# Taking two more chunks of the first layer's activations off TensorE's transposes and through DRAM

## The chip, the cores and the metric

The kernel runs on one NeuronCore of one Trainium2 chip. The metric is device time in microseconds (us) for one execution; lower is better. TensorE (PE) does the matrix products and can also transpose, VectorE (DVE), ScalarE (ACT) and GpSimd (POOL) do element work, and SyncE (SP) issues most of the DMAs.

## What is computed

The input x has 64 batches of 32 channels by 512. Four residual layers follow each other. The first is the largest: a gated feed-forward layer with low-rank adapters chosen per batch.

```python
def L0(x, W_gate, W_up, W_down, A_gate, B_gate, A_up, B_up, A_down, B_down, ids):
    gate = x @ W_gate.T + 0.5 * adapters(x, A_gate, B_gate, ids)     # F = 1376 columns
    up   = x @ W_up.T   + 0.5 * adapters(x, A_up, B_up, ids)
    act  = silu(gate) * up
    return act @ W_down.T + 0.5 * adapters(act, A_down, B_down, ids)

x = x + L0(x, ...)
x = x + einsum('bct,bcd->bdt', x, L1_weights[cond])      # a 32 x 32 mix of the channels
x = x + L2(x, ...)     # x @ W.T, a router over 8 experts (top 2), rank-16 experts
x = x + einsum('bct,bcd->bdt', x, L3_weights[cond])
```

All data is float32. Each product is made of three matmuls of split operands (high times high, high times low, low times high), so every operand of a product is first written as a high part (ScalarE, L901) and a low part (VectorE, L1126).

## The kernel before

The 2048 rows of x are 16 tiles of 128 rows. In the first layer each tile's 1376 columns are cut into three chunks: n = 0 has 352 columns, n = 1 and n = 2 have 512. A pair of tile and chunk is a step, s = 3i + n from the seventh step on, and there are 48 steps, 0 to 47. In a step TensorE computes gate and up into PSUM (`gate`, `up`, `adapters`), ScalarE applies Silu, VectorE multiplies, and the activations go to SBUF. The down product contracts over the chunk's columns, so the activations must be transposed first. There are two ways to do that.

- On TensorE: `transpose_act(d)` turns up to four 128 x 128 blocks into the PSUM tile act_t (L1473), from which ScalarE and VectorE make the two parts.
- In squares, for the steps in MOVED, 4 to 44 before the change: behind the product `blocks(s)` on VectorE turns each 32 x 32 square in place (L1172) into act_blk, `move_act(d)` on SyncE stores act_blk to DRAM (L702, 256 KB), waits for the store to land (L708), and loads it back with four DMAs that put the squares where they belong (L710, 64 KB each) into x_res[:, 1], from which the parts are made. ScalarE and VectorE make those parts a step later than the others, and TensorE's `down` follows two steps behind the gate.

The order of the work on each engine is written out by hand. `lane_jobs(s)` is the order that ScalarE and VectorE share: the job ("act", d) makes the parts of chunk d, ("gate", s) is Silu and product, ("b", s) the parts of gathered adapters, ("tdm", i) and ("td", i) the down adapters' operand, ("x1", i) the residual sum. TensorE's order is the loop over steps at the end of its block. SyncE goes through its own loop over s; at s = 46 it waits for step 45's sums (s_gu), issues the weights of L2 (four DMAs of 324 KB, L732) and three block-diagonal matrices of L1 and L3 (256 KB each, L696), and at s = 47, after step 46's sums, b2 (L737) and five more matrices. Within one s, `move_act(s - 1)` stands behind those loads. At s = 47 the residual tile is stored and a fresh one loaded (L655, L755), and then the first tiles of the second layer (L686).

Around the end of the first layer the engines also begin the second. Before ("gate", 47) ScalarE splits the weights of L2 (`high_w2`, L1040) and a tile of L1; VectorE does `take_x2(0)` and two `low_w2`, and after the gate two more `low_w2` and `low_x2t(0)`. TensorE runs `l1(0)` inside step 47's up, `transpose_x2(0)` after its adapters, and then down(45), down(46), transpose_act(47) and the first product of L2.

The step's activations stand in act[:, 0] or act[:, 1] by turns; for a step in MOVED they stand in act[:, 1] and act_blk is act[:, 0]. So step MOVED[-1] + 1, whose Silu writes act[:, 0], first waits on ScalarE until the last block has been stored (s_aout).

Of the kernel before, what the change touches and what calls it, by code (L numbers as in the profile page):

```python
# [59 lines left out]
STEPS = NT * NC  # L60
# [16 lines left out]
def cw(f):  # L77

    return min(P, F - f * P)


def width(n):
    return CHUNKS[n][1] - CHUNKS[n][0]


def pieces_of(n):

    return range(CHUNKS[n][0] // P, -(-CHUNKS[n][1] // P))
# [34 lines left out]

MOVED = range(4, STEPS - 3)


MOVED_X2 = 3
# [6 lines left out]
def step_of(i, n):  # L136
    return ORDER.index((i, n))
# [19 lines left out]
def pe_transposed(d):  # L157

    return sum(k not in MOVED for k in range(d + 1))

# [11 lines left out]
def wgu_items(n, m):  # L172
    return [("wgu", n, m, c) for c in range(HC)]


def wd_items(n):
    return [("wd", f) for f in pieces_of(n)]


def first_items():  # L180

    w = wgu_items(0, 0)
    return [("x", 0, 0), w[0], w[1], ("x", 0, 1), w[2], w[3], ("x", 1, 0)] + wgu_items(0, 1)
# [41 lines left out]
def lane_jobs(s):  # L225

    if s <= FREE:
        w1u, w2g, w2u = wgu_items(1, 1), wgu_items(2, 0), wgu_items(2, 1)
        return {-1: first_items(),
                0: (wgu_items(1, 0) + [("at", 0)] + w1u[:2] + [("b", 0), w1u[2], ("tm", 0), w1u[3], ("t", 0), ("b", 1),
                    ("tc", 0), w2g[0], ("gate", 0), w2g[1], ("at", 1)]),
                1: w2g[2:] + [("gate", 1), ("tm", 1)] + w2u[:2] + [("t", 1)] + w2u[2:] + [("tc", 1)],
                2: [("b", 2), ("adt", 0), ("b", 3), ("adt", 1), ("gate", 2), ("act", 0)] + wd_items(0),
                3: [("gate", 3)] + wd_items(1) + [("act", 1), ("b", 4)],
                4: wd_items(2) + [("act", 2), ("gate", 4), ("bd", 0), ("b", 5), ("x", 2, 0)],  # L240
                5: [("tdm", 0), ("td", 0), ("act", 3), ("x1", 0), ("at", 2), ("gate", 5), ("b", 6)],
                6: [("act", 4), ("tm", 2), ("t", 2), ("adt", 2), ("gate", 6), ("b", 7)]}[s]
    i, n = divmod(s, NC)
    last = [("act", s - 1)] if s - 1 not in MOVED else []
    if i == NT:
        return last + [("bd", i - 1), ("tdm", i - 1), ("td", i - 1), ("x1", i - 1)]
    acts = ([("act", s - 2)] if s - 2 in MOVED else []) + last
    if n == 0:
        return [("tm", i)] + acts + [("t", i), ("gate", s), ("b", s + 1)]
    if n == 1:  # L250
        x = [("x", i + 1, 0)] if i + 1 < NT else []
        return acts + x + [("bd", i - 1), ("gate", s), ("tdm", i - 1), ("b", s + 1), ("td", i - 1)]
    jobs = acts[:1] + [("x1", i - 1)] + acts[1:]
    if i + 1 < NT:
        return jobs + [("at", i + 1), ("gate", s), ("b", s + 1), ("adt", i + 1)]
    return jobs + [("gate", s)]
# [6 lines left out]
def bass_conditioned_residual_chain(nc, x_t, x_rows, it_cond, it_lang, wgu, wd, a_all, a_gu, a_d, b_d,  # L263
# [6 lines left out]
    with ExitStack() as ctx:  # L270
        def sb(name, shape, dt=F32, stack=ctx):
            return stack.enter_context(nc.sbuf_tensor(name, [P, *shape], dt))
# [52 lines left out]
        act = sb("act", [2, H], F32, mem_a)  # L325
# [32 lines left out]
        x1 = sb("x1", [2, H])  # L358
# [181 lines left out]
        def act_of(s):  # L540
            w = width(ORDER[s][1])
            if s in MOVED:
                return act[:, 1, 0:w]
            return act[:, slot(s), 0:w] if slot(s) < 2 else x_res[:, 1, 0:w]
# [10 lines left out]
        def moved(d):  # L555

            return d - MOVED[0] + 1

# [82 lines left out]
        def s_lo_of(job):  # L641
            return split_no[job]
# [9 lines left out]
        def _(sp):  # L652
# [46 lines left out]
            def move_act(d):  # L699

                sp.wait_ge(s_blocks, moved(d))
                sp.dma_start(act_scratch[d % 2, :, :], act_blk).then_inc(s_aout, 16)  # L702
                if d - 1 in MOVED:
                    sp.wait_ge(s_lo, s_lo_of(("act", d - 1)))
# [689 lines left out]
        def _(pe):  # L1394
            def product(out_, stationary, moving, start, stop):

                pe.matmul(out_, stationary[0], moving[0], start=start, stop=False, skip_group_check=True)  # L1397
                pe.matmul(out_, stationary[0], moving[1], start=False, stop=False, skip_group_check=True)  # L1398
                return pe.matmul(out_, stationary[1], moving[0], start=False, stop=stop, skip_group_check=True)  # L1399
# [17 lines left out]
            def gate(s, c0, c1):  # L1417
                i, n = ORDER[s]
                out_ = gate_of(s) if n or i < 2 else bank(s, 0)[:, 0:AW + GATE0]
                if c0 == 0 and slot_before(s) is not None:  # L1420
                    pe.wait_ge(s_mul, slot_before(s) + 1)
                if c0 == 0 and n == 0 and i >= 1:
                    pe.wait_ge(s_lo, s_lo_of(("x", i, 0)))
                if c0 == 0 and n == 0 and i >= 2:
                    pe.wait_ge(s_lo, s_lo_of(("at", i)))
                for c in range(c0, c1):
                    if i == 0:
                        pe.wait_ge(s_lo, s_lo_of(("wgu", n, 0, c)))
                        if n == 0 and c % 2 == 0:
                            pe.wait_ge(s_lo, s_lo_of(("x", 0, c // 2)))  # L1430
                    mm = product(out_, x_of(i, c), gate_moving(i, n, c), c == 0, False)
                if n == 0 and i >= 2 and c1 == HC:
                    mm.then_inc(s_tx, 1)

            def up(s, c0, c1):
                i, n = ORDER[s]
                for c in range(c0, c1):
                    if i == 0:
                        pe.wait_ge(s_lo, s_lo_of(("wgu", n, 1, c)))
                    product(up_of(s), x_of(i, c), wgu_parts(n, 1, c)[1:], c == 0, False)  # L1440
# [21 lines left out]
            def transpose_act(d):  # L1462
                i, n = divmod(d, NC)
                s = step_of(i, n)
                pe.wait_ge(s_mul, s + 1)
                if d == 0:
                    pe.wait_ge(s_ident, 16)
                before = max((k for k in range(d) if k not in MOVED), default=None)
                if before is not None:
                    pe.wait_ge(s_lo, s_lo_of(("act", before)))  # L1470
                for j, f in enumerate(pieces_of(n)):
                    w = cw(f)
                    mm = pe.transpose(act_t[0:w, j, :], act_of(s)[:, j * P:j * P + w], ident)  # L1473
                mm.then_inc(s_actt, 1)

            def down(d):
                i, n = divmod(d, NC)
                pe.wait_ge(s_lo, s_lo_of(("act", d)))
                if d == 0:
                    pe.wait_ge(s_mul, step_of(1, 0) + 1)  # L1480
                if n == 0:
                    pe.wait_ge(s_lo, s_lo_of(("adt", i)))
                    if i >= 1:
                        pe.wait_ge(s_x1, i)
                at = i % 2 * AD_HALF
                for j, f in enumerate(pieces_of(n)):
                    w = cw(f)
                    if i == 0:
                        pe.wait_ge(s_lo, s_lo_of(("wd", f)))
                    a_hl = [act_hl[0:w, d % 2, part, j, :] for part in range(2)]  # L1490
                    for half in range(2):
                        mm = product(down_ps[:, half, 0:D_COLS], a_hl,
                                     [wd_sb[0:w, f, part, half, at:at + D_COLS] for part in range(2)],
                                     n == 0 and j == 0, False)
                mm.then_inc(s_d, 1)
# [127 lines left out]
            for s in range(FREE + 1, STEPS):  # L1623
                i, n = ORDER[s]
                finishes = n == 2
                gate(s, 0, HC // 2)
                gate(s, HC // 2, HC)
                if s > MOVED[-1] + 1:
                    transpose_act(s - 1)
                up(s, 0, HC // 2)  # L1630
                if finishes:
                    down_adapters(i - 1)
                if s == STEPS - 1:
                    l1(0)
                up(s, HC // 2, HC)
                if n > 0:
                    adapters(s)
                if s == STEPS - 1:
                    transpose_x2(0)
                if s - 2 in MOVED:  # L1640
                    down(s - 2)
                if n == 0:
                    adapters(s)
            down(STEPS - 3)
            down(STEPS - 2)
            transpose_act(STEPS - 1)
            l2_base(0, 1)
# [99 lines left out]
```

## Time and profile before

| | us |
|---|---|
| median of 3 runs | 550.65 |
| lowest, highest | 550.13, 554.97 |
| profiled execution, device time | 551.23 |
| its span | 549.4 |
| PE busy in the span | 539.2 (98%) |
| PE weight load busy | 488.5 (89%) |
| DVE busy | 330.6 (60%) |
| ACT busy | 209.7 (38%) |
| POOL busy | 212.8 (39%) |

The span is what the profiler saw of one execution from its first to its last instruction. An execution takes 1.8 us more than its span, and the profiled one took 0.6 us more than the median. TensorE's granted clock is full in all 40 slices of the page. The chain that ended last is 96% TensorE.

### The profile page before, as it was taken

Reading aid. Unit: us, or ns where it says so; the run is one execution under the profiler, and the core shown is the slowest. Engines: PE = TensorE matmul, PEld = TensorE weight load, DVE = VectorE, ACT = ScalarE, POOL = GpSimd, SP = SyncE. Lnnn points to the kernel's source line nnn. Section 1 sums busy time; section 2 is a strip of 40 time slices with the busy share of each in tenths; the row PEclk is TensorE's granted clock in tenths of the full one; section 3 lists DMA queues with packets and bytes.
Section 4 is the critical chain, followed back from the end, with each engine's and each line's share of the span. In section 5 each row is a group of like instructions: output and inputs, shape, how many; then the busy total and the mean of one; then the engine's idle time right before and its main releaser. Section 6 shows DMA issues by size and latency. Waiting matters only on the chain.

```text
span 549.4 us, 8715 instructions
## 1 busy us (share of the span) xinstructions
PE 539.2 (98%) x3120; PEld 488.5 (89%) x3120; DVE 330.6 (60%) x775; ACT 209.7 (38%) x418; POOL 212.8 (39%) x236
## 2 busy tenths in 40 slices
PE   5999999999999999999999999999999999999997
PEld 5879989898989898989898989898989899999996
DVE  5788554645564646564555455545554577777765
ACT  6675242424242424242333323232323543444432
POOL 4743244746584757433232323241412342121100
PEclk9999999999999999999999999999999999999999
DMA  8985555666667666655555555564555832667642
GB/s 287 374 254 201 163 180 177 190 209 197 207 199 221 184 219 190 229 171 190 161 179 164 177 164 177 163 184 161 186 164 169 299 116 92 214 212 227 229 140 76
DMA packets 73466, 105.71 MB, mean 192 GB/s; under 512 B 9552, under 2 KB 40912, under 8 KB 73424
## 3 DMA queue, kind: packets, MB, share of 16 engines
q1 hardware_dynamic: 62400, 67.87, 37.6%
q0 software_dynamic: 10880, 37.23, 22.2%
q8 instruction: 24, 0.39, 0.3%
q14 instruction: 18, 0.15, 0.1%
q10 hardware_dynamic: 144, 0.06, 0.0%
HBM read 78.39 MB, written 26.74 MB: 191 GB/s over the span
## 4 chain that ended last, share of the span: by engine, by line
PE 96%; DVE 2%; DMA 1%; ACT 1%; issue 0%; SPq 0%; DVEq 0%; ACTq 0%
PE gu_ps L1397 15%; PE gu_ps L1399 15%; PE gu_ps L1398 15%; PE down_ps L1397 9%; PE down_ps L1398 9%; PE down_ps L1399 9%; PE l_ps L1397 5%; PE l_ps L1398 5%; PE l_ps L1399 5%; PE gu_ps L1404 3%; PE gu_ps L1405 3%; PE down_ps L1405 1%; PE down_ps L1404 1%; DMA wg_sb_raw<-wgu 1%; PE act_t L1473 0%; DVE wd_sb L1126 0%
## 5 line engine op out<-in xcount | busy, mean ns | idle before, releaser
L798 POOL DMA_INDIRECT b_sel_raw<-b_gu,idx_rank x48 | 46.3, 965 | 153.3 <-PE gu_ps L1405 135.2
L1397 PE MATMUL down_ps<-wd_sb,act_hl 128*128 128x288 f32 (+1 forms) x352 | 103.9, 295 | 0.3 <-DVE wd_sb L1126 0.3
L1398 PE MATMUL down_ps<-wd_sb,act_hl 128*128 128x288 f32 (+1 forms) x352 | 103.7, 295 | 0.0
L1399 PE MATMUL down_ps<-wd_sb,act_hl 128*128 128x288 f32 (+1 forms) x352 | 103.6, 294 | 0.0
L1397 PE MATMUL gu_ps<-w_sb,xt 128*128 128x512 f32 x256 | 101.1, 395 | 0.2 <-DVE act L1199 0.2
L1399 PE MATMUL gu_ps<-w_sb,xt 128*128 128x512 f32 x256 | 100.0, 391 | 0.0
L1398 PE MATMUL gu_ps<-w_sb,xt 128*128 128x512 f32 x256 | 100.0, 391 | 0.0
L1199 DVE TENSOR_TENSOR act<-act,gu_ps 128x512 f32<-128x512 f32 (+1 forms) x47 | 29.8, 634 | 106.7 <-ACT act L926 106.7
L926 ACT ACTIVATE act<-gu_ps 128x512 f32<-128x512 f32 (+1 forms) x47 | 26.2, 556 | 176.9 <-PE gu_ps L1405 176.9
L798 POOL DMA_INDIRECT a_raw<-a_all,idx_batch x60 | 70.2, 1170 | 54.0 <-DVE wd_sb L1126 39.9
L1397 PEld LDWEIGHTS down_ps<-wd_sb,act_hl 128*128 128x128 f32 (+1 forms) x352 | 66.0, 188 | 2.2 <-DVE wd_sb L1126 0.7
L1398 PEld LDWEIGHTS down_ps<-wd_sb,act_hl 128*128 128x128 f32 (+1 forms) x352 | 66.1, 188 | 1.2
L1399 PEld LDWEIGHTS down_ps<-wd_sb,act_hl 128*128 128x128 f32 (+1 forms) x352 | 66.0, 188 | 0.0
L1399 PEld LDWEIGHTS gu_ps<-w_sb,xt 128*128 128x128 f32 x256 | 48.1, 188 | 10.6
L1397 PEld LDWEIGHTS gu_ps<-w_sb,xt 128*128 128x128 f32 x256 | 48.1, 188 | 9.0 <-DVE act L1199 0.6
L1398 PEld LDWEIGHTS gu_ps<-w_sb,xt 128*128 128x128 f32 x256 | 48.2, 188 | 8.2
L1126 DVE TENSOR_TENSOR b_sel<-b_sel_raw,b_sel 128x1024 fp32r<-128x1024 f32 (+1 forms) x48 | 52.2, 1088 | 3.4 <-ACT b_sel L901 3.3
L862 POOL TENSOR_TENSOR x_hl<-x,x_hl 128x512 fp32r<-128x512 f32 x16 | 21.8, 1360 | 67.9 <-ACT x_hl L1032 67.9
L901 ACT CAST b_sel<-b_sel_raw 128x1024 fp32r<-128x1024 f32 (+1 forms) x48 | 45.7, 952 | 0.9 <-DMA b_sel_raw<-b_gu,idx_rank 0.9
L1397 PE MATMUL l_ps<-w2ra_hl,x2t_hl 128*128 128x328 f32 (+1 forms) x128 | 41.6, 325 | 0.0
L1398 PE MATMUL l_ps<-w2ra_hl,x2t_hl 128*128 128x328 f32 (+1 forms) x128 | 39.8, 311 | 0.0
L1399 PE MATMUL l_ps<-w2ra_hl,x2t_hl 128*128 128x328 f32 (+1 forms) x128 | 39.5, 309 | 0.0
(165 smaller groups left out, 1057.6 us busy)
## 6 DMA issues: line engine op xcount, KB each, us to landing
act_blocks<-act SPq DMA_DIRECT2D x41, 256.0 KB, 4.2
x_res<-act_blocks SPq DMA_DIRECT2D x164, 64.0 KB
xt_raw<-x_t SPq DMA_DIRECT2D x16, 256.0 KB, 5.0
w_sb_raw<-wgu SPq DMA_DIRECT2D x16, 256.0 KB, 7.9
x_res<-x_rows SPq DMA_DIRECT2D x16, 256.0 KB, 2.8
x_after_l<-x_res SPq DMA_DIRECT2D x16, 256.0 KB, 2.2
bd<-bd_hl SPq DMA_DIRECT2D x16, 256.0 KB
x<-x_after_l SPq DMA_DIRECT2D x16, 256.0 KB, 2.9
```

The source lines that it names most:

```text
L798: nc.gpsimd.indirect_dma_start(out=dst, out_offset=None, in_=table, in_offset=bass.IndirectOffsetOnAxis(ap=idx, axis=0)).then_inc(s, 16)
L862: pool.tensor_tensor(x1_hl[:, t % 2, 1, :], x1[:, t % 2, :], x1_hl[:, t % 2, 0, :].bitcast(F32), ALU.subtract).then_inc(s_x1lo, 1)
L901: sc.copy(out_, in_).then_inc(s_hi, 1)
L926: sc.activation(act_of(s), gate_of(s), ACT.Silu).then_inc(s_silu, 1)
L1126: return ve.tensor_tensor(out_, raw, high.bitcast(F32), ALU.subtract)
L1199: ve.tensor_tensor(a, a, up_of(s), ALU.mult).then_inc(s_mul, 1)
L1397: pe.matmul(out_, stationary[0], moving[0], start=start, stop=False, skip_group_check=True)
L1398: pe.matmul(out_, stationary[0], moving[1], start=False, stop=False, skip_group_check=True)
L1399: return pe.matmul(out_, stationary[1], moving[0], start=False, stop=stop, skip_group_check=True)
L1404: pe.matmul(out_, stationary, moving[0], start=False, stop=False, skip_group_check=True)
L1405: return pe.matmul(out_, stationary, moving[1], start=False, stop=True, skip_group_check=True)
```

## The change

MOVED takes in steps 45 and 46, so that only step 47 of the late steps is transposed on TensorE. In the job order the parts of chunks 45 and 46 are made one step later than before, and down(45) moves in TensorE's code from after the loop into its last turn, which is the same place in TensorE's order.

```diff
-MOVED = range(4, STEPS - 3)
+MOVED = range(4, STEPS - 1)
...
     last = [("act", s - 1)] if s - 1 not in MOVED else []
     if i == NT:
-        return last + [("bd", i - 1), ("tdm", i - 1), ("td", i - 1), ("x1", i - 1)]
+        return [("act", s - 2)] + last + [("bd", i - 1), ("tdm", i - 1), ("td", i - 1), ("x1", i - 1)]
...
                 gate(s, 0, HC // 2)
                 gate(s, HC // 2, HC)
-                if s > MOVED[-1] + 1:
-                    transpose_act(s - 1)
                 up(s, 0, HC // 2)
...
                 if n == 0:
                     adapters(s)
-            down(STEPS - 3)
             down(STEPS - 2)
             transpose_act(STEPS - 1)
             l2_base(0, 1)
```

The same constants steer the helpers that are not in the diff: `move_act(45)` and `move_act(46)` are now issued by SyncE, `blocks(45)` and `blocks(46)` run on VectorE, `act_of` puts steps 45 and 46 in act[:, 1], and it is ("gate", 47) on ScalarE that waits for all stores of blocks.

## Rows read from the trace of the kernel before

**Rows 1.** Waits of the whole kernel on PE, the longest

```profile
PE gu_ps L1397 <- DVE wg_sb L1126: 5.8, 1, 5.8
```

**Rows 2.** Busy time by stretch (window, PE, PEld, DVE, ACT, POOL, clock, DMA share, GB/s)

```profile
433.00:437.00 4.00, 4.00 (x21) 3.33 (x21) 3.17 (x6) 1.43 (x4) 1.39 (x1) 1.00 1.00 383
437.00:441.00 4.00, 4.00 (x21) 3.31 (x21) 3.35 (x7) 2.98 (x5) 0.94 (x1) 1.00 0.19 71
```

**Rows 3.** Timeline of PE (start, us) through the last steps

```profile
429.68 0.40 PE L1397 MATMUL down_ps<-wd_sb,act_hl 128*128 128x288 f32 x1
...
435.70 0.60 PE L1473 MATMUL act_t<-ident_sb,act 128*128 128x128 f32 x4
...
436.37 0.39 PE L1398 MATMUL gu_ps<-w_sb,xt 128*128 128x512 f32 x1
...
437.52 0.28 PE L1404 MATMUL down_ps<-bd_hl,td_hl 128*128 128x256 f32 x1
...
441.32 0.38 PE L1397 MATMUL down_ps<-wd_sb,act_hl 128*128 128x288 f32 x1
...
443.80 0.30 PE L1397 MATMUL down_ps<-wd_sb,act_hl 128*128 128x288 f32 x1
```

**Rows 4.** Timeline of SyncE's issues (start, us), merged

```profile
381.70 1.73 SPq L710 DMA_DIRECT2D x_res<-act_blocks  x4
...
424.64 1.86 SPq L732 DMA_DIRECT2D w2ra_hl_raw<-w2ra_t  x4
426.55 1.78 SPq L696 DMA_DIRECT2D bd_hl<-bd  x3
429.73 0.33 SPq L737 DMA_DIRECT2D b_hl_raw<-b  x1
430.11 2.36 SPq L696 DMA_DIRECT2D bd_hl<-bd  x5
```

**Rows 5.** DMA issues, 424 to 437.5 us (last number: us to landing)

```profile
b_hl_raw<-b SPq DMA_DIRECT2D x1, 256.0 KB, 4.9
```

**Rows 6.** The last of the eight matrix loads, by its tile

```profile
L696 SPq DMA_DIRECT2D bd_hl<-bd x1: 431/431/431, 432.0 to 432.0; - x1
...
DMA to landing us min/median/max: 5.8/5.8/5.8
```

**Rows 7.** The page's DMA issues, median us to landing

```profile
x<-x_after_l SPq DMA_DIRECT2D x16, 256.0 KB, 2.9
```

**Rows 8.** The second layer's 52 loads of squares (64 KB each), L769

```profile
DMA to landing us min/median/max: 1.8/2.5/4.3
```

**Rows 9.** Timeline of ACT (start, us)

```profile
428.28 0.62 ACT L901 CAST act_hl<-x_res 128x512 fp32r<-128x512 f32 x1 [3.89 <-DMA x_res<-act_blocks]
...
436.82 2.64 ACT L1040 CAST w2ra_hl<-w2ra_hl_raw 128x648 fp32r<-128x648 f32 x4
...
441.16 0.60 ACT L926 ACTIVATE act<-gu_ps 128x512 f32<-128x512 f32 x1 [1.18 <-PE gu_ps L1405]
```

**Rows 10.** Timeline of DVE (start, us)

```profile
413.65 0.71 DVE L1172 STREAM_TRANSPOSE act<-act 128x512 f32<-128x512 f32 x1
...
428.94 0.69 DVE L1126 TENSOR_TENSOR act_hl<-x_res,act_hl 128x512 fp32r<-128x512 f32 x1 [3.29 <-ACT act_hl L901]
...
434.43 1.31 DVE L1126 TENSOR_TENSOR td_rows<-t_m,td_rows 128x64 fp32r<-128x64 f32 x1
...
443.11 1.56 DVE L1126 TENSOR_TENSOR w2ra_hl<-w2ra_hl_raw,w2ra_hl 128x648 fp32r<-128x648 f32 x2
444.60 0.68 DVE L1257 TENSOR_TENSOR x2t_hl<-x2t_ps,x2t_hl 128x512 fp32r<-128x512 f32 x1
```

**Rows 11.** Timeline of POOL (start, us)

```profile
434.26 1.39 POOL L862 TENSOR_TENSOR x_hl<-x,x_hl 128x512 fp32r<-128x512 f32 x1 [1.69 <-ACT x_hl L1032]
```

**Rows 12.** PE alone by stretch, at the kernel's first matmuls

```profile
5.79:10.94 5.15, 5.15 (x17) 1.00 0.96 330
10.94:16.00 5.06, 5.06 (x33) 1.00 1.07 387
```

## The prediction

> **What bounds the kernel now.** I read the page first: TensorE is busy 98% of the span, and the chain that ended last is TensorE's own for 96%. Then its waits over the whole kernel: the longest is the one ahead of the first matmul, 5.8 us [rows 1]; every other is below 1 us. Then the busy time by stretch around the edit: TensorE is busy all of 433 to 441 us, while the DMA engines, which the page shows half idle, are saturated at 383 GB/s until 437 and nearly idle after it [rows 2]. So a microsecond taken from TensorE's stream is a microsecond of the kernel, a transfer costs nothing as long as it lands before TensorE asks, and the stretch of this edit is the one where transfers don't land soon. Last I read the timelines of SyncE, ScalarE, VectorE and GpSimd there, for the order in which things would now be late.
>
> **What goes.** Seven TensorE transposes, three for chunk 45 and four for chunk 46. The four start at 435.70 and the second matmul behind them at 436.37, 0.67 us; a 512-column matmul takes 0.23 (five from 436.37 to 437.52), so they cost 0.44 [rows 3]. The three would be 0.33 in proportion, but they give nothing: down(44), which comes behind them, starts at 429.68 and VectorE's low part of chunk 44 at 428.94, behind ScalarE's at 428.28, which waited for a DMA [rows 3, 9, 10]; TensorE would only wait there. So 0.44 us is the whole saving. The parts read from PSUM give way to parts read from SBUF at about the same price.
>
> The Trainium skill weighs the same swap ("VectorE: DVE Perf Modes", The three transpose paths): TensorE 390 ns for a 128 x 128 bf16 block, VectorE 311 ns but in 32 x 32 blocks only, and its advice for a full block whose result may lie in PSUM is TensorE, which speaks against the change. By its figure seven blocks would give back 2.7 us; the rows price four at 0.44, and they decide.
>
> **What comes in, and where it queues.** Blocks(45) and blocks(46) cost VectorE at most 0.71 us each [rows 10]; it has room. The transfers decide. I follow SyncE.
>
> (a) SyncE issues the four weight loads and three matrices from 424.64 to 428.33 [rows 4]. Move_act(45) stands behind them: its store goes out at 428.4, though its block is ready by about 425. b2, behind the same seven in the trace of before, went out at 429.73 and landed 4.9 later, at 434.63 [rows 4, 5]. The store takes about that place in the line: 434.5. A store was not seen behind such loads, so bounds: 430.2, if it overtook them (the shortest landing of rows 8, 1.8), and 434.6 and a bit.
>
> (b) SyncE waits for the store, issues four loads in 1.73 us, 434.55 to 436.3 [rows 4], the last at 435.85. It lands 2.5 later, 438.4 (between 1.8 and 4.3) [rows 8]. All this time b2 and five matrices, which before went out at 429.73, are held back.
>
> (c) They go out from 436.35 to 439.1, the same 2.74 us as before [rows 4]. Move_act(46) stands behind them too: store at 439.15. The first of the line lands 2.9 after its issue, as a 256 KB load does mostly [rows 7], 439.25. Before, from b2's landing at 434.63 to the last matrix's at 432.05 + 5.8 = 437.85, five transfers took 3.2, 0.64 each [rows 5, 6]. Five matrices and the store: 439.25 + 6 x 0.64 = 443.1. Bounds: 439.15 + 1.8 = 440.95 and 439.15 + 5.8 = 444.95.
>
> (d) Four loads again: the last goes out 1.3 later, 444.4, and lands at 446.9 (bounds from 440.95 + 1.3 + 1.8 = 444.05 to 444.95 + 1.3 + 4.3 = 450.55).
>
> (e) ScalarE's high part, VectorE's low part 0.66 behind it, TensorE 0.74 behind that, as for chunk 44 [rows 3, 9, 10]: down(46) starts at 448.3. Before it started at 443.80 [rows 3]. Sum: +4.5 us, and the 0.44 is inside it, since TensorE gains nothing by coming early to a wait. The whole stream of TensorE behind it is in order and full, so nothing makes up for it.
>
> **Waits on the way, and who stands behind them.** VectorE: blocks(46) waits until store 45 has landed, 434.5, where before VectorE went on to ("tdm", 14), ("b", 47) and ("td", 14). The low part of td_rows then starts about 436.7 and not 434.43. Before, this 128x64 operation took 1.31 us and ended when GpSimd's operation of 434.26 ended [rows 10, 11]; ScalarE's work for that one is behind ("td", 14) and moves too, so it can be caught again. td_hl is ready about 438.5, and down_adapters(14), which TensorE would reach at 437.52 - 0.44 = 437.1 [rows 3], waits about 1.4 us. That makes adapters(47) end 1.0 later, about 442.0. ScalarE: part 45 begins at 438.4, where part 46 began at about the same place before; the weights' high parts (2.64) and one of 0.62 bring it to 442; Silu 47, at 441.16 before [rows 9], now waits for store 46, 443.1. VectorE behind it: product 47, two low_w2 (1.56), low_x2t [rows 10] end about 446.6, just before part 46 lands. These delays lie before 448.3 and cost nothing of their own; they set a floor. If store 46 landed at once, Silu would start at 442.0, VectorE be through at about 445.5, its low part of chunk 46 start there and down(46) 0.74 later at 446.2: +2.4. SyncE: the residual tile and the second layer's first tiles go out at about 445 to 448 and not 439 to 442; their users stand behind down(46) and move with it.
>
> **The sum against the profiled execution:** 551.23 + 4.5 = 555.7. That execution is 0.58 above the median, so the predicted median is 550.65 + 4.5 = 555.2 us, 0.8% slower.
>
> **Rivals.**
> 1. The forecast: the line of loads holds both stores back, down(46) waits about 3.5 us. 555.2, between 553.5 and 556.8. Chance 0.60.
> 2. TensorE's clock falls in that wait. For it: after the 5.8 us without work at the start, 17 recorded matmuls took 5.15 us and the next 33, nearly all of the same size, 5.06 [rows 1, 12], though the granted clock stood at 1.00: the rate of the lower level, 1.2 GHz, and then that of the upper, 2.4. That cost 17 x (0.303 - 0.153) = 2.5 us. Against it: the wait here is shorter (down(45) takes 443.80 - 441.32 = 2.5 us from about 442.3, so TensorE is idle from 444.8 to 448.3) [rows 3]. 555.2 + 2.5 = 557.7. Chance 0.15. The Trainium skill ("TensorE: Matmul & The Clock Gate", Part 1: The HAM clock gate) has the clock fall to 1.2 GHz after an idle stretch and rise after sustained work; by that rule the trace's start agrees, and the end of this wait could go the same way.
> 3. The landings come at their long ends (443.1 + 1.9, last load 4.3 instead of 2.5): up to +8.2, 558.8; in the middle of that, 557. Chance 0.12.
> 4. Stores don't queue behind the loads, and VectorE's order is last: +2.4, 553.1. Chance 0.08.
> 5. The other side: everything lands before it is asked for, because the SyncE order hardly matters and ScalarE and VectorE run ahead. Then only the transposes count: -0.44, 550.2, no slower. It decides if part 46 lands before about 442, for which store 46 would have to go out before 438; SyncE sits in the wait for store 45 until then. Chance 0.05, a gain over 1% in none of the cases; 0.01 for what I don't see.
>
> **Range and chances.** A measurement of this kernel tells about 1% (5.5 us) from no change. Cases 1, 4 and 5 lie within it, but for the upper end of case 1, 0.07; cases 2 and 3 and that end are slower by over 1%, 0.34. Same 0.65, faster 0.01. For 8 in 10 I leave out case 5 and part of 4 below and the far end of 3 above: 552.7 to 558.2.
>
> **What the changed profile would show.** Store 45 issued near 428.4 and landed near 434.5, store 46 near 439.2 and 443; SyncE's waits at L708 long for both; b2 at about 436. A wait of TensorE at down_adapters(14) of about 1 us, and one before down(46) of about 3.5, released by VectorE's low part of chunk 46 and that by a DMA. Silu 47 released by a DMA. Matmul spacing behind the wait tells case 2: 0.14 us for 288 columns at the upper level (18 of down(45) in 2.48) [rows 3], about double at the lower. The forecast is wrong if store 45 lands before 432, if SyncE issues b2 before 433, or if TensorE's wait ends with ScalarE or VectorE busy on other work up to then.

## The result and the profile after

| | before | after |
|---|---|---|
| median of 6 runs each | 553.56 us | 560.15 us |
| ratio | | 1.013, 95% interval 1.0084 to 1.0176 |
| profiled execution, device time | 551.23 | 560.21 |
| its span | 549.4 | 558.1 |

The change makes the kernel about 7 us slower. The forecast was 0.8%, 4.5 us. Whole runs of one kernel scatter by several us here, much of it from waits long before the place of the edit (TensorE stood still for 3.2 us at 25 us in e1, for 3.8 near 160 us in e8), so what follows is measured in profiles from one instruction that all of them have: the start of Silu of step 45, which lies between 422.98 and 435.73 us in them. From it to the end of the span the kernel before took 549.4 - 422.99 = 126.4 us and the changed one 558.1 - 423.64 = 134.5, 8.1 more.

TensorE's longest waits over the whole changed kernel (engine, line, waited for: us in total, times, longest):

```profile
PE down_ps L1397 <- DVE act_hl L1126: 6.6, 2, 5.9
PE gu_ps L1397 <- DVE wg_sb L1126: 5.6, 1, 5.6
PE down_ps L1404 <- DVE td_hl L1238: 1.3, 1, 1.3
```

The second is the one of [rows 1]. The other two are new (0.7 us of the first row lie at 44 us and are not of this place), and there was no wait of TensorE in this place before. Where they come from is in SyncE's timeline, which answers to [rows 4]:

```profile
423.63 2.52 SPq L732 DMA_DIRECT2D w2ra_hl_raw<-w2ra_t  x4
426.19 2.38 SPq L696 DMA_DIRECT2D bd_hl<-bd  x3
428.62 0.67 SPq L702 DMA_DIRECT2D act_blocks<-act  x1
435.19 1.74 SPq L710 DMA_DIRECT2D x_res<-act_blocks  x4
436.98 0.43 SPq L737 DMA_DIRECT2D b_hl_raw<-b  x1
437.46 2.33 SPq L696 DMA_DIRECT2D bd_hl<-bd  x5
439.83 0.43 SPq L702 DMA_DIRECT2D act_blocks<-act  x1
446.00 1.75 SPq L710 DMA_DIRECT2D x_res<-act_blocks  x4
```

Each store (L702) stands behind a line of loads, each as large as the store or larger, and SyncE issues nothing until it has landed: from 428.62 + 0.67 to 435.19, and from 439.83 + 0.43 to 446.00. ScalarE's timeline, beside [rows 9], shows who waits for that:

```profile
439.44 0.51 ACT L901 CAST act_hl<-x_res 128x384 fp32r<-128x384 f32 x1 [2.40 <-DMA x_res<-act_blocks]
...
446.02 0.60 ACT L926 ACTIVATE act<-gu_ps 128x512 f32<-128x512 f32 x1 [3.01 <-DMA act_blocks<-act]
...
449.83 0.62 ACT L901 CAST act_hl<-x_res 128x512 fp32r<-128x512 f32 x1 [2.74 <-DMA x_res<-act_blocks]
```

Silu of step 47 waits for store 46, and the high part of chunk 46 for its four loads. VectorE's low part follows, and then TensorE, beside [rows 3]:

```profile
438.57 0.39 PE L1404 MATMUL down_ps<-bd_hl,td_hl 128*128 128x256 f32 x1 [1.30 <-DVE td_hl L1238]
...
451.23 0.61 PE L1397 MATMUL down_ps<-wd_sb,act_hl 128*128 128x288 f32 x1 [5.92 <-DVE act_hl L1126]
451.63 0.44 PE L1398 MATMUL down_ps<-wd_sb,act_hl 128*128 128x288 f32 x1
...
454.27 0.31 PE L1397 MATMUL down_ps<-wd_sb,act_hl 128*128 128x288 f32 x1
454.42 0.29 PE L1398 MATMUL down_ps<-wd_sb,act_hl 128*128 128x288 f32 x1
...
455.88 0.60 PE L1473 MATMUL act_t<-ident_sb,act 128*128 128x128 f32 x4
```

Twelve matmuls start from 451.23 up to 454.27, 0.25 apart; from 454.27 on they are 0.13 apart. The busy times of PE by stretch (window and its length, PE busy with its matmuls, granted clock, DMA share, GB/s) say why:

```profile
446.00:447.00 1.00, 0.00 (x0) 1.00 0.63 82
447.00:448.00 1.00, 0.00 (x0) 0.73 0.66 243
...
450.00:455.00 5.00, 3.77 (x18) 0.57 0.45 161
455.00:460.00 5.00, 5.00 (x36) 1.00 0.00 0
```

The granted clock fell to 0.5, the lower level of 1.2 GHz, while TensorE stood still, and rose to 1.00, 2.4 GHz, in the middle of down(46). Down(46) took 455.88 - 451.23 = 4.65 us and not 447.01 - 443.80 = 3.2 as before, where transpose_act(47) started at 447.01.

Side by side, in us behind Silu of step 45 (the yardstick is the changed kernel's second profile, on another chip):

| | before | forecast | after | yardstick |
|---|---|---|---|---|
| store 45 landed | | 11.5 | 11.5 | 11.8 |
| b2 issued | 6.7 | 13.4 | 13.3 | 13.6 |
| store 46 issued | | 16.2 | 16.2 | 16.6 |
| store 46 landed | | 20.1 | 22.3 | 22.3 |
| down(46) starts | 20.8 | 25.3 | 27.6 | 27.1 |
| end of the span | 126.4 | 130.9 | 134.5 | 134.6 |

The chain is the forecast's up to the second store, to 0.1 us. Two things were not in its sum: 2.2 us in the second line, and what the clock cost, which is the 1.3 us (134.5 - 27.6 against 126.4 - 20.8, so 106.9 against 105.6) that the kernel took longer from the start of down(46) on; down(46) by itself took 1.4 longer.

### The profile page after: what moved, and what is told of

The parts are those of the page before. It is cut to its first block, busy times and chain, and to the rows that moved or that the text cites. A ratio compares the mean times of both kernels' runs of the same rounds, so it can differ in the third digit from the quotient of the medians.

```text
span 558.1 us, 8714 instructions
## 1 busy us (share of the span) xinstructions
PE 540.3 (97%) x3113; PEld 488.9 (88%) x3113; DVE 331.6 (59%) x777; ACT 210.4 (38%) x417; POOL 208.3 (37%) x236
## 4 chain that ended last, share of the span: by engine, by line
PE 89%; DMA 6%; SPq 2%; DVE 1%; issue 0%; ACT 0%; POOL 0%; DVEq 0%
PE gu_ps L1397 13%; PE gu_ps L1399 13%; PE gu_ps L1398 13%; PE down_ps L1397 8%; PE down_ps L1398 8%; PE down_ps L1399 8%; PE l_ps L1397 5%; PE l_ps L1398 5%; PE l_ps L1399 5%; PE gu_ps L1404 3%; PE gu_ps L1405 3%; DMA act_blocks<-act 2%; DMA wd_sb_raw<-wd 1%; DMA b_sel_raw<-b_gu,idx_rank 1%; SPq L696 1%; PE down_ps L1405 1%
## 5 line engine op out<-in xcount | busy, mean ns | idle before, releaser
L798 POOL DMA_INDIRECT a_raw<-a_all,idx_batch x60 | 68.3, 1139 | 53.9 <-DVE wd_sb L1126 39.9
```

Of the source, the lines that this page charges most:

```text
L798: nc.gpsimd.indirect_dma_start(out=dst, out_offset=None, in_=table, in_offset=bass.IndirectOffsetOnAxis(ap=idx, axis=0)).then_inc(s, 16)
```

## The experiments

Theory 1: the stores stand in line behind the loads that SyncE issues ahead of them, and everything follows from that order. Theory 2: the way through DRAM (store, wait, four loads) is itself too long at this place. Theory 3: ScalarE and VectorE reach part 46 too late in their own order. Each kernel is the changed one with the edit shown; where a store or a move is issued earlier, its old place in SyncE's loop leaves it out, which the cuts don't show. Its time is given as the ratio to the kernel before on the same chip (b0, e9 and e6 are one execution each and have none), and its profile, one for each run, from Silu of step 45 to the end of the span.

**The yardstick** (a0_after), the changed kernel unedited.

> The changed kernel as it is, as a yardstick on the chip of the next three. Every theory expects 6 to 8 us over the kernel before. It also tells whether store 46's 6.1 us from issue to landing is this kernel's or that one execution's: if the line of loads alone sets it, 6.1 again within 0.5; if the dip in DMA rate around 441 us was chance, between 4 and 6.

Ratio 1.0188 (1.0133 to 1.0243), 564.67 against 556.16 us. From Silu of step 45 (425.03) to the end (559.6): 134.6. PE's waits repeat:

```profile
PE down_ps L1397 <- DVE act_hl L1126: 5.4, 1, 5.4
PE down_ps L1404 <- DVE td_hl L1238: 1.5, 1, 1.5
```

Store 46 went out at 441.62 and its loads at 447.31, 5.7 us. So the long landing repeats and is not that of one execution.

**The stores ahead of the loads** (e1_stores_first).

```diff
                 if s == STEPS - 2:
                     sp.wait_ge(s_gu, chunk_done(0))
+                    store_act(s - 1)
                     for c in range(HC):
...
                 if s == STEPS - 1:
                     sp.wait_ge(s_gu, chunk_done(1))
+                    store_act(s - 1)
                     sp.dma_start(w2_parts(HC)[0], b2).then_inc(s_w[HC], 16)
```

> In the changed kernel SyncE issues the store of block 45 ahead of the weights of L2, and that of block 46 ahead of b2, and the loads of squares stay where they are. Theory 1 (the stores stand in line behind the loads issued ahead of them): store 45 lands within 3 us of its issue, b2 goes out at 431 to 433 again, part 46 lands before 442, TensorE doesn't wait at all, and the time is that of the kernel before, -1 to +1 us. Theory 2 (the way through DRAM is itself too long, whatever the order): still +3 us or more, with a wait before down(46). Theory 3 (part 46 comes too late in ScalarE's and VectorE's order): +2 to +3 us, the wait ending with VectorE busy.

Ratio 1.0013 (0.9973 to 1.0053), 556.9 us, and 555.2 - 427.42 = 127.8 from Silu of step 45. SyncE's timeline there:

```profile
429.15 0.34 SPq L701 DMA_DIRECT2D act_blocks<-act  x1
429.53 2.35 SPq L736 DMA_DIRECT2D w2ra_hl_raw<-w2ra_t  x4
431.93 1.62 SPq L696 DMA_DIRECT2D bd_hl<-bd  x3
434.36 1.74 SPq L713 DMA_DIRECT2D x_res<-act_blocks  x4
436.35 0.34 SPq L701 DMA_DIRECT2D act_blocks<-act  x1
436.73 0.43 SPq L742 DMA_DIRECT2D b_hl_raw<-b  x1
```

b2 goes out 9.3 us behind Silu of step 45 instead of 13.3. By the ratio no loss can be told from none; by the profiles 6.7 of the 8.1 us are back (134.5 - 127.8) and 1.4 are left. That is theory 1, and theory 2, which expected 3 us or more whatever the order, can't be the main cause. This profile has no landing time for the two stores; in e8, with the same order, each landed 4.0 us behind its issue and not within 3, against 6.5 and 6.1 in the changed kernel and a median of 4.2 (2.4 to 5.6) for the 41 stores of blocks in the kernel before. So more than half of what the first store gains is that SyncE needn't issue seven loads before it: it goes out 1.7 us behind Silu of step 45 (429.15 - 427.42) and not 5.0 (428.62 - 423.64). I was wrong to expect no wait at all: two are left, 2.0 us together, the longer 1.4 us before down(46). VectorE is busy right up to it:

```profile
446.18 0.67 DVE L1204 TENSOR_TENSOR act<-act,gu_ps 128x512 f32<-128x512 f32 x1
446.77 1.56 DVE L1131 TENSOR_TENSOR w2ra_hl<-w2ra_hl_raw,w2ra_hl 128x648 fp32r<-128x648 f32 x2
448.26 0.68 DVE L1262 TENSOR_TENSOR x2t_hl<-x2t_ps,x2t_hl 128x512 fp32r<-128x512 f32 x1
448.86 0.67 DVE L1131 TENSOR_TENSOR act_hl<-x_res,act_hl 128x512 fp32r<-128x512 f32 x1
```

So theory 3 comes in second place: VectorE's order sets what is next once the transfers are early. e8 tries that.

**Only the second block ahead of its loads** (e2_46_first).

```diff
                 if s == STEPS - 1:
                     sp.wait_ge(s_gu, chunk_done(1))
+                    move_act(s - 1)
                     sp.dma_start(w2_parts(HC)[0], b2).then_inc(s_w[HC], 16)
```

> In the changed kernel the whole move of block 46 (store, wait, four loads) goes ahead of b2 and the five matrices; the move of block 45 stays behind the weights of L2 and three matrices. Theory 1: store 45 lands at 434 to 435 as before, store 46 goes out at 437 and lands within 3 us, so the second line's share (3 to 4 us of the landing) is gone: the wait before down(46) falls from 5.9 to 1 to 2 us, TensorE's clock doesn't fall, down_adapters(14) still waits its 1.3 us; +1.5 to +3 us over the kernel before. Theory 2: the wait stays over 4 us. If the loss sits in the first line, +5 us or more.

Ratio 1.0086 (1.0047 to 1.0124), 129.5 from Silu of step 45: +3.1, as expected or just above; the ratio says +4.8 (2.6 to 6.9). The wait before down(46) is 1.7 us, with VectorE busy right up to it, and the clock stayed at 1.00 behind it. By the profiles the second line makes about 5 of the 8.1 us and what is left, 3, is the first line with VectorE's order.

**Only the first block ahead of its loads** (e3_45_first).

```diff
                 if s == STEPS - 2:
                     sp.wait_ge(s_gu, chunk_done(0))
+                    move_act(s - 1)
                     for c in range(HC):
                         sp.dma_start(w2_parts(c)[0], w2ra_t[c * P:(c + 1) * P, :]).then_inc(s_w[c], 16)
```

> In the changed kernel the whole move of block 45 goes ahead of the weights of L2 and the three matrices; the move of block 46 stays behind b2 and the five matrices. If the line costs where the block stands in it: store 45 lands within 3 us, VectorE's blocks(46) and down_adapters(14) wait for nothing, the weights of L2 are put off by 5 us and b2 with them, so the second line is as long as ever and store 46 stands at its end behind all of both: it lands 445 to 447 on the clock of the changed kernel, and the wait before down(46) stays at 4 to 6 us. So +5.5 to +8 us over the kernel before: moving the first block alone gives nothing back. Rival (the delay of the first store passes on to the second): the wait before down(46) shrinks by the 4 us that store 45 gains.

Ratio 1.0086 (1.0043 to 1.0129), 559.6 - 424.19 = 135.4 from Silu of step 45, so in that execution no better than the changed kernel. The ratio of the ten runs says otherwise: +4.7 us on 551.54 (2.4 to 7.1), below what I expected, half of the profile's +9.0, and below the whole interval of the yardstick's. Whether moving the first block alone gives nothing back, as the profile has it, or some 3 us, as the runs have it, stays open. In the profile store 45 landed 4.4 us behind its issue, not within 3, and store 46 22.6 us behind Silu of step 45, where it landed in the changed kernel. What one wait gave back another took, which I had not foreseen (waits behind Silu of step 45):

```profile
PE down_ps L1398 <- DVE act_hl L1127: 4.1, 2, 3.4
PE l_ps L1398 <- POOL x_hl L863: 2.8, 1, 2.8
```

With the weights of L2 put off, GpSimd's work on them is late, and the low part of x1 behind it on GpSimd's queue, for which TensorE waits inside step 47. The granted clock stayed at 1.00 in that wait of 2.8 us; in the one before down(46), 3.4 us, it fell.

**Work in place of the wait, 33 matmuls** (e4_filler).

```diff
+            a_old = [act_hl[:, (STEPS - 3) % 2, part, 0, :] for part in range(2)]
+            for _ in range(11):
+                product(l3_ps[:, 0:D_COLS], a_old, [wd_sb[:, 8, part, 0, 0:D_COLS] for part in range(2)], True, False)
             down(STEPS - 2)
```

> The changed kernel with 33 matmuls of 288 columns more, which write into a PSUM bank that nothing reads yet, between down(45) and down(46), 4.4 us of work where TensorE waited 5.9. They add nothing if the wait is DMA's. If the clock's fall cost 1.3 us as the spacing says (12 matmuls of down(46) at 0.24 against 0.13), the first matmuls of down(46) are 0.13 apart and the kernel is 1.0 to 1.5 us faster than the changed one. Rival: the wider spacing behind the wait is a cost of restarting and not of the clock, or the shortened wait of 1.5 us makes the same fall; then the same time as the changed kernel.

Ratio 1.0221 (1.016 to 1.0282), 135.2 from Silu of step 45. It isn't faster: 2.3 us without work were left, and the clock fell all the same, behind the wait (PE busy by stretch):

```profile
446.00:450.00 4.00, 4.00 (x32) 1.00 0.56 185
450.00:453.00 3.00, 0.69 (x6) 1.00 0.10 31
453.00:456.50 3.50, 3.50 (x17) 0.53 0.65 220
```

Down(46) took 457.56 - 452.74 = 4.8 us.

**The same with 45 matmuls** (e5_filler_long; `range(15)` for `range(11)`).

> As the filler of 33, which left 2.3 us of idle time in which the granted clock still fell, but with 45 matmuls (5.9 us), so that TensorE hardly stops before down(46). If the clock's fall costs 1.3 us: no wait over 1 us there, granted clock 1.00 over the next 5 us, the 24 matmuls of down(46) in 3.2 us and not 4.6, and from Silu of step 45 to the end of the span 0.5 to 1.3 us less than in the changed kernel (134.5). If the fall came of something else than the idle time, 134.5 again and the clock at 0.5.

The clock stayed up:

```profile
445.00:450.00 5.00, 5.00 (x40) 1.00 0.52 159
450.00:453.00 3.00, 1.65 (x13) 1.00 0.25 83
453.00:456.50 3.50, 3.50 (x29) 1.00 0.42 156
```

Down(46) took 455.00 - 451.70 = 3.3 us, and down(46) to the end of the span 557.6 - 451.7 = 105.9, 1.0 less than in the changed kernel. So the slow matmuls are the clock's and not a cost of starting again behind a wait, and filling the idle time keeps the clock up. That idle time's length alone decides is not shown: the wait of 2.3 us in e4 brought a fall, one of 2.8 in e3 none. The stretch from Silu of step 45 is 134.6 nevertheless, and my expectation of a gain over the changed kernel fails: part 46 landed late in that execution (its high part started 27.3 us behind Silu, 26.2 in the changed kernel), so that down(46) started 28.7 behind and not 27.6. The ratio, 1.0139 (1.0071 to 1.0207), can't tell 1 us.

**A shorter second line** (e7_short_line).

```diff
                     sp.dma_start(w2_parts(HC)[0], b2).then_inc(s_w[HC], 16)
-                    for t in range(3, BD):
+                    for t in range(3, 5):
                         load_bd(t)
...
                     move_act(s - 1)
+                if s == STEPS - 1:
+                    for t in range(5, BD):
+                        load_bd(t)
```

> In the changed kernel three of the five matrices go behind the move of block 46, so that its store has b2 and two matrices ahead of it and not b2 and five. By the line with 0.64 us a transfer: store 46 lands 1.9 us sooner against Silu of step 45 (22.3 behind it in the changed kernel, then 20.4), the wait before down(46) falls from 5.4 to 5.9 to 3.5 to 4, and 132.5 from Silu of step 45 to the end (134.5 in the changed kernel). If the 2 us over my price were a slower rate of every transfer (1 us each), it gains 3 us; if they come once in each line that starts anew, 1.9 and the slow stretch stays.

Ratio 1.0099 (1.006 to 1.0138), 557.7 - 427.44 = 130.3 from Silu of step 45, 4.2 less than the changed kernel, twice what I priced. (The ratio says +5.5 us, 3.3 to 7.6, on the kernel before; the profile +3.9.) Store 46 landed 19.4 us behind Silu, 2.9 sooner (its loads went out at 446.83), the wait before down(46) was 2.3 us, and the clock didn't fall (1.00 from 451 to 456), which accounts for the other 1.3. Three transfers fewer gave 2.9 and not 1.9 us. That is the number of the rival, 1 us each, but the landings don't say so: two of three behind b2 came 0.6 and 0.7 apart, one 1.2.

**The matrices from another place in DRAM** (e6_other_source).

```diff
-                             bd_scratch[t, :, :]).then_inc(s_bdin[t % BD], 16)
+                             x_scratch[t * P:(t + 1) * P, :] if 3 <= t < BD else bd_scratch[t, :, :]
+                             ).then_inc(s_bdin[t % BD], 16)
```

> The changed kernel with matrices 3 to 7 read from rows of the first layer's result in DRAM instead of the matrices' own scratch, so that the channel mixes of tiles 3 to 7 and all of their second layer are not the reference's. It asks why the five matrices and the store took 5.5 to 6 us behind b2 instead of 3.8. If it is where they are read from: 0.64 us a transfer, store 46 lands 20.5 us behind Silu of step 45. If each line that starts anew pays for it: 5.3 us or more again, store 46 at 22.

Store 46 landed 448.41 - 426.04 = 22.4 us behind Silu of step 45, the wait before down(46) was 5.5. Two of its matrix loads, one behind the other (line, count, duration, start; then us to landing):

```profile
L696 SPq DMA_DIRECT2D bd_hl<-x_after_l x1: 430/430/430, 440.3 to 440.3; - x1
...
DMA to landing us min/median/max: 2.8/2.8/2.8
```

```profile
L696 SPq DMA_DIRECT2D bd_hl<-x_after_l x1: 430/430/430, 440.7 to 440.7; - x1
...
DMA to landing us min/median/max: 4.9/4.9/4.9
```

They landed at 443.1 and 445.6, 2.5 us apart and not 0.64. In the changed kernel the same loads, the first and the second of the five:

```profile
L696 SPq DMA_DIRECT2D bd_hl<-bd x1: 430/430/430, 437.5 to 437.5; - x1
...
DMA to landing us min/median/max: 3.4/3.4/3.4
```

```profile
L696 SPq DMA_DIRECT2D bd_hl<-bd x1: 430/430/430, 437.9 to 437.9; - x1
...
DMA to landing us min/median/max: 4.6/4.6/4.6
```

That is 440.9 and 442.5, 1.6 apart, and the next at 444.0 (5.6 behind its issue at 438.4); then 0.6 each. With another source the slow stretch is there again, so where they are read from is not its cause, as far as one execution tells. In the one line that never ran dry, e3's from the weights of L2 to store 46, the weights landed 1.9 and 1.3 apart at its start and all that followed 0.6 to 0.75 apart. So most lines seen here have one slow stretch near their start, 1 to 2.5 us; what makes it is open.

**Part 46 early, on top of the stores first** (e8_part46_early).

```diff
-        return [("act", s - 2)] + last + [("bd", i - 1), ("tdm", i - 1), ("td", i - 1), ("x1", i - 1)]
+        return last + [("bd", i - 1), ("tdm", i - 1), ("td", i - 1), ("x1", i - 1)]
...
-    return jobs + [("gate", s)]
+    return jobs + [("gate", s), ("act", s - 1)]
```

> As the kernel with the stores ahead of the loads (556.9 us, 1.4 us of wait before down(46), behind two low_w2 and low_x2t on VectorE), but the parts of chunk 46 are made right behind the gate of step 47 and ahead of those. If VectorE's order is what the wait ends on: the wait before down(46) is below 0.3 us, 126.4 or less from Silu of step 45 to the end (127.8 in that kernel, 126.4 in the one before), and the time equals the kernel before within noise, at best 0.4 us faster. If the landing is last: the wait stays above 1 us. Rival: low_x2t comes too late instead, and the wait moves to the first product of L2.

Ratio 1.0011 (0.9975 to 1.0048), 552.8 against 551.54 us. In its profile TensorE has no wait behind Silu of step 45 (429.21), and the stretch is 554.5 - 429.21 = 125.3, 1.1 us less than the kernel before. With the two low_w2 and low_x2t out of its way the wait is gone, so VectorE's order is what the 1.4 us were. Two more profiles were to tell whether the 1.1 us hold.

> The kernel before once more, for its profile. From Silu of step 45 to the end of the span it took 126.4 us, the kernel with the stores first and part 46 early 125.3. If that stretch repeats within 0.3 us, 126.1 to 126.7, it can tell the 0.8 us of seven transposes where the time of a whole run can't.

551.0 - 424.82 = 126.2: it repeats within 0.3.

> The kernel with the stores first and part 46 early once more, for its profile: 125.0 to 125.7 us from Silu of step 45 to the end if its 1.1 us under the kernel before are the transposes (0.44 + 0.33) and the wait they covered; 126 or more if they were chance.

563.6 - 435.73 = 127.9, and not 125.0 to 125.7. Here part 46 landed late again, ScalarE idle before it, and TensorE waited 0.9 us:

```profile
455.17 0.62 ACT L906 CAST act_hl<-x_res 128x512 fp32r<-128x512 f32 x1 [1.63 <-DMA x_res<-act_blocks]
```

Its other waits behind Silu of step 45, at the experts of the second layer, are 0.6. That leaves 0.2 us of the difference to b0 unexplained and 1.1 of that to e8. So the stretch was 1.1 shorter than before in one profile and 1.5 longer in the other, and a saving is not shown. Over whole runs no version beat the kernel before.

## Why the prediction was wrong, point by point

It had the sign and the mechanism, and too small a size: +4.5 us, where the ratio says +7.2 (4.6 to 9.7) and the profiles +8.1.

- **What goes:** right that the changed kernel keeps nothing of the transposes, wrong on the way there. The forecast had the three of chunk 45 give nothing, since part 44 would come too late. In the changed profile part 44 was early enough (its high part at 426.35, 2.7 us behind Silu of step 45; before 5.3), down(44) started 6.2 behind Silu and not 6.7, and TensorE reached down_adapters(14) at 438.57 - 1.30 = 437.27, 13.6 behind Silu where the kernel before had 14.5. So 0.9 us had been gained by then (0.7 against b0, which had no stall at down(44)), and the wait of 1.3 took it all.
- **(a), (b), where the first store stands:** right to 0.1 us, landing at 11.5 and b2 issued at 13.3 behind Silu of step 45.
- **(c), the second line: this step failed, and with it the sum.** I priced it at 0.64 us a transfer, read from b2 and the last matrix [rows 5, 6], the tail of a line that had been running for eight transfers. Behind b2 the six transfers took 5.5 to 6.0 us and not 3.8, and store 46 landed 22.3 us behind Silu of step 45 and not 20.1. The trace of before had a sign of it, a weak one: the first of the weights of L2 went out at 424.64 [rows 4] and the line there lost time near its start too (the second, issued at 425.1, landed at 429.8, the third, issued at 425.6, at 431.2: 1.4 us apart, for 324 KB, which at 0.64 for 256 KB would be 0.8). My bound for the landing, 5.8 us from issue, was also the old line's; it measured 6.1 and 5.7.
- **(d), (e):** right. From store 46's landing to down(46) it took 5.3 us in the changed kernel; forecast 5.2.
- **Waits on the way:** the one at down_adapters(14), forecast 1.4, measured 1.3. The one before down(46), forecast 3.5, measured 5.9, by (c). That the first costs nothing of its own is borne out by the table, in which down(46) is where the transfers put it.
- **Rival 2, the clock,** had a chance of 0.15 and happened, for 1.3 us (forecast 2.5); it is the rest of what the sum lacked: 4.5 + 2.2 + 1.3 = 8.0 of 8.1. I took the wait as short against the 5.8 us at the start; e3 shows the clock fall in a wait of 3.4, as long as the one forecast, and e4 in one of 2.3. It should have been in the likeliest case.
- **Rival 4,** VectorE's order as a floor at +2.4, is what e2 shows (+3.1) and e1 and e8 single out (1.4 us before down(46)). Its price was about right, but it needed the loads out of the way.
- **Rivals 3 and 5:** the landing's long end was nearer the truth than its 0.12, though by the line and not by the single transfers. Part 46 landing before it is asked for was seen only with the stores first, in e8, and not in e9. (The chances add up to 1.01.)

## What to carry to other kernels

A transfer that something waits for goes ahead of the bulk loads on its queue; two stores issued earlier gave back 6.7 of the 8.1 us, and all that the whole runs can tell. When a queue is stopped by a wait for its own store, the loads behind it are held too and start a new line, so price that line as one that starts, from landings near the start of one, and not at the settled rate. And a wait of TensorE of 2 us or more is to be priced with a chance that the clock falls behind it.

## What I had not expected of the hardware

- The granted clock fell in or right behind waits of TensorE of 5.9, 5.5, 5.4, 3.4 and even 2.3 us (after, e6, yardstick, e3, e4), and did not in waits of 2.8, 2.3, 1.7, 1.4 and 1.4 (e3 at 442, e7, e2, e1, e5). Far from the edit it fell behind a wait of 1.9 us too (e6, TensorE idle until 24.05, the clock at 0.50 from 25 to 28). So from about 2 to 3 us the length of the wait alone doesn't tell. The Trainium skill ("TensorE: Matmul & The Clock Gate", Part 1: The HAM clock gate) has it fall after idle time; these waits agree in kind, and between e4 and e7 the same length went both ways.
- A line of DMAs had a slow stretch of 1 to 2.5 us near its start, in most lines of these profiles (in e8's it was under 1 us), whether the loads read one place in DRAM or another.
